# First projection of a perceiver kernel: DMA order, fold products and key loads rearranged

## The reference

```
q_hk  = (layernorm(x) @ Wq.T).reshape(b, s, H, K)          # H=16, K=128
q_big = einsum('bshk,hkq->bshq', q_hk, w_kc_q)             # 192
q_r   = einsum('bshq,hqr->bhsr', q_big, W_qr)              # 64
k_r   = einsum('bld,hdr->bhlr', kv_rope, W_kr)
scores = einsum('bhsr,bhlr->bhsl', q_r, k_r)
...
out = ctx_lat.reshape(b, s, H * K) @ Wo.T
```

## Time and profile before

| | us |
|---|---|
| three runs, median (lowest to highest) | 834.14 (825.74 to 835.28) |
| the profiled execution | 835.64 |
| its span | 833.9 |
| first projection: from the span's start to the first product of the next stage | 78.7 |

### The profile page before, as it was taken

One profiled execution on the slowest core, in us unless ns is written; L12 is line 12 of the kernel. 1 busy time (PEld: TensorE's weight loads), 2 busy tenths in 40 slices (PEclk: granted clock), 3 DMA queues, 4 the chain that ended last, 5 costly groups with the idle time before them and its releaser, 6 DMA issues. The chain is left out here.

```text
span 833.9 us, 16002 instructions
## 1 busy us (share of the span) xinstructions
PE 705.1 (85%) x5490; PEld 471.9 (57%) x5490; DVE 591.0 (71%) x1151; ACT 426.2 (51%) x1314; POOL 369.4 (44%) x312
## 2 busy tenths in 40 slices
PE   4996999788457569899996899769999999999776
PEld 3664666478313345443442577447777776777644
DVE  3456778565778646566675788598888888888477
ACT  1455788244157511222233777326655555668764
POOL 3400454152426313433476544246666676667200
PEclk9999899999569758999999899899999999999999
DMA  8454000000020002252010000002222233231001
GB/s 241 133 150 157 2 2 2 0 2 1 0 89 1 0 21 88 76 164 89 0 39 1 1 1 2 1 20 58 59 57 57 58 99 100 58 107 22 1 1 52
DMA packets 33572, 41.92 MB, mean 50 GB/s; under 512 B 15072, under 2 KB 23264, under 8 KB 32608
## 3 DMA queue, kind: packets, MB, share of 16 engines
q1 hardware_dynamic: 33504, 41.06, 16.8%
HBM read 40.00 MB, written 1.05 MB: 49 GB/s over the span
## 5 line engine op out<-in xcount | busy, mean ns | idle before, releaser
L1918 POOL TENSOR_TENSOR ra_direct<-ra_direct,ra_crossed 128x512 f32<-128x512 f32 x64 | 81.2, 1269 | 80.0 <-DVE ra_crossed L2094 80.0
L695 POOL TENSOR_TENSOR c_probs<-c_probs,c_inverse 128x512 f32<-128x512 f32 x64 | 65.7, 1041 | 74.3 <-DVE c_inverse L711 74.3
L2094 DVE SCALAR_TENSOR_TENSOR ra_crossed<-bank,ra_bias,ra_sin 64x512 f32<-64x512 f32 x128 | 96.0, 750 | 1.9
L1383 POOL TENSOR_TENSOR r_turned<-r_times_a,r_times_b 128x1024 f32<-128x1024 f32 x24 | 56.4, 2350 | 86.2 <-DVE r_times_b L1582 86.2
L670 ACT ACTIVATE c_probs<-bank,c_neg_max 128x128 f32<-128x128 f32 x256 | 90.2, 391 | 5.3 <-DVE c_neg_max L729 5.3
L670 ACT ACTIVATION_READ_ACCUMULATOR c_probs<-bank,c_neg_max 128x1 f32 x256 | 59.4, 232 | 0.0
L2046 ACT ACTIVATE ra_probs_t<-bank 64x256 f32<-64x256 f32 x64 | 24.2, 377 | 59.8 <-PE bank L1988 59.4
L1661 POOL TENSOR_TENSOR ra_w_lo<-ra_raw,ra_w_hi 128x768 f16<-128x768 f32 x32 | 52.7, 1646 | 0.0
L2052 ACT ACTIVATE ra_probs<-ra_masked,ra_neg_max 128x64 f32<-128x64 f32 x128 | 42.9, 336 | 18.5 <-DVE ra_neg_max L2114 18.3
L58 PE MATMUL bank<-xt_hi,ra_w_hi 128*128 128x512 f16 x128 | 49.3, 385 | 1.6 <-DVE ra_crossed L2094 0.9
L621 PE MATMUL bank<-c_probs_t,c_keys 128*64 128x512 f32 x128 | 37.3, 663 | 14.0 <-DVE c_probs_t L721 11.8
(11 more groups left out here) (248 smaller groups left out, 2099.3 us busy)
## 6 DMA issues: line engine op xcount, KB each, us to landing
ra_raw<-l_attn_w_dram SPq DMA_DIRECT2D x32, 384.0 KB, 3.1
wq<-l_wq_dram SPq DMA_DIRECT2D x16, 256.0 KB, 2.9
wo<-l_wo_dram SPq DMA_DIRECT2D x16, 256.0 KB, 3.4
wkcq<-l_wkcq_dram SPq DMA_DIRECT2D x16, 192.0 KB, 3.1
ra_wo<-l_attn_wo_dram SPq DMA_DIRECT2D x1, 2048.0 KB, 9.9
wqr<-l_wqr_dram SPq DMA_DIRECT2D x16, 96.0 KB, 3.3
x_res<-x_dram SPq DMA_DIRECT2D x2, 512.0 KB, 4.7
wkv<-l_wkv_dram SPq DMA_DIRECT2D x16, 64.0 KB, 2.8
```

Source lines behind the costliest of these rows:

```text
L695: nc.gpsimd.tensor_tensor(out=probs[u][:, at, :], in0=probs[u][:, at, :], in1=inverse[u][:, at].unsqueeze(2).broadcast_to([P, HP, L]), op= ...
L1383: nc.gpsimd.tensor_tensor(out=turned[k % 3][:], in0=times_a[k % 2][:], in1=times_b[k % 2][:], op=ALU.add).then_inc(rotated, 1)
L1918: nc.gpsimd.tensor_tensor(out=direct[e][k][:], in0=direct[e][k][:], in1=crossed[k][:], op=ALU.add).then_inc(roped, 1)
L2094: ins = nc.vector.scalar_tensor_tensor(dst[out_lo:out_lo + rows].rearrange("p t (b s) -> p (t b) s", b=2), src[lo:lo + rows], bias[e][lo:l ...
```

## The change

- SyncE loads the weights of pair 0 first, then the two halves of x (each with a semaphore of its own) and the identity, then pair 1.
- Step n of TensorE is now B(n+1), p(n,0), M(n+1), O(n+1), A(n+2), p(n,1). A(1) stands ahead of the steps, behind the first eight transposes; the other eight stand behind p(0,0). ScalarE's and VectorE's orders follow.
- The three loads for the keys stand behind the weights of pair 3, the eleven of the attention weights behind those of pair 4. The first keys are transposed behind step 5 instead of step 1.
- All eight steps are written out; there is no loop any more. VectorE takes the statistics of the first half of x when that half is there, and stores fold product 0 between the two scalings.

```diff
-def pair_loop(eng, step):
...
+def pair_loop(step):
+
+    for n in range(PAIRS):
+        step(n, n % 2, n // 2, n + 1 < PAIRS)
...
-        KEY_GROUPS = {1: (0, 1), PAIRS - 2: (2, 3)}
+        KEY_GROUPS = {PAIRS - 3: (0, 1), PAIRS - 2: (2, 3)}
...
+            for n in range(PAIRS):
+                u = n % 2
                 wait(sp, m_done, n - 1)
                 wait(sp, o_done, n - 1)
                 for dst, name in ((wqr, "l0_wqr"), (wkr, "l0_wkr"), (wkcq, "l0_wkcq"), (wq, "l0_wq"),
                                   (wkv, "l0_wkv"), (wo, "l0_wo")):
                     sp.dma_start(dst[u][:], a[name][n]).then_inc(loaded[u], 16)
-                if isinstance(n, int) and n == 1:
+                if n == 0:
+                    for q in range(2):
+                        rows = slice(q * TH, (q + 1) * TH)
+                        sp.dma_start(m.x[:, rows, :], x_in[:, rows, :]).then_inc(x_loaded[q], 16)
+                    sp.dma_start(m.ident[:], a["ident"]).then_inc(ident_loaded, 16)
+                if n == 3:
                     keys.sync(sp)
+                if n == 4:
                     prep.load(sp)
...
                 if more:
-                    multiply_a(n + 1, v, i + u)
+                    multiply_b(n + 1, v)
                 project(n, u, 0)
+                if isinstance(n, int) and n == 0:
+                    for k in (2, 3):
+                        ln.transpose(pe, k)
                 if more:
-                    multiply_b(n + 1, v)
+                    multiply_m(n + 1, v)
                     multiply_o(n + 1, v)
-                    multiply_m(n + 1, v)
+                if later(n):
+                    multiply_a(n + 2, u, i + 2)
                 project(n, u, 1)
...
-            ln.tensor(pe)
-            pair_loop(pe, step)
+            for k in (0, 1):
+                ln.transpose(pe, k)
+            multiply_a(1, 1, 1)
+            pair_loop(step)
...
-            dve.wait_ge(x_loaded, 32)
-            ln.vector(dve)
+            for q in range(2):
+                dve.wait_ge(x_loaded[q], 16)
+                ln.statistics(dve, q)
+            ln.scale(dve, 0)
+            keep_o(0)
             keep_m(0, 0)
-            keep_o(0)
-            pair_loop(dve, step)
+            ln.scale(dve, 1)
+            for k in (0, 1):
+                ln.low(dve, k)
+            pair_loop(step)
```

More of the change, by code:

```diff
@@ L380, in cross_project_plain, with later @@
         ln = normalise_steps(nc, g, "ln0")
-        x_loaded, ident_loaded = g.sem("x_loaded"), g.sem("ident_loaded")
+        x_loaded, ident_loaded = [g.sem(f"x_loaded{q}") for q in range(2)], g.sem("ident_loaded")
         block = own.enter_context(nc.Block())
+        def later(n):
+            return not isinstance(n, int) or n + 2 < PAIRS
         @block.gpsimd
@@ L405, in step @@
                     sp.dma_start(dst[u][:], a[name][n]).then_inc(loaded[u], 16)
-                if isinstance(n, int) and n == 1:
+                if n == 0:
[4 more added lines that the diff above has]
+                if n == 3:
                     keys.sync(sp)
+                if n == 4:
                     prep.load(sp)
-            pair_loop(sp, step)
             load_ffn_weights(nc, g, sp)
@@ L413, in _, with multiply_a @@
         def _(pe):
-            def multiply_a(n, u, i):
-                pe.wait_ge(loaded[u], 16 * LOADS * (i + 1))
+            def multiply_a(n, u, trips):
+                pe.wait_ge(loaded[u], 16 * LOADS * trips)
                 wait(pe, a_kept, n)
@@ L470, in step @@
                     keys.tensor(pe, KEY_GROUPS[n])
-            multiply_a(0, 0, 0)
+            multiply_a(0, 0, 1)
             multiply_o(0, 0)
@@ L503, in step @@
                 if more:
-                    keep_a(n + 1)
+                    keep_b(n + 1)
                 lat.high(act, n, u, 0)
+                if isinstance(n, int) and n == 0:
+                    for k in (2, 3):
+                        ln.high(act, k)
                 if more:
-                    keep_b(n + 1)
+                    keep_m(n + 1, v)
                     keep_o(n + 1)
-                    keep_m(n + 1, v)
+                if later(n):
+                    keep_a(n + 2)
                 lat.high(act, n, u, 1)
@@ L517, in _ @@
             keep_m(0, 0)
-            ln.scalar(act)
-            pair_loop(act, step)
+            for k in (0, 1):
+                ln.high(act, k)
+            keep_a(1)
+            pair_loop(step)
         @block.vector
```

## The result

Over 20 runs of each, the changed kernel has a median of 836.8 us (833.0 to 843.3), the one before 833.6 (825.7 to 841.1). The ratio is 1.0061, 95% interval 1.0036 to 1.0085: slower by 3.2 us between the medians and by some 5 us by the ratio, which leaves out runs in a slower state of the chip. That is well under 2%, but clear of the noise. A gain of 0.5 us was forecast. The ratios further down are to the kernel before too, with the same kind of interval, each against runs of it that were made beside them.

The account below looks back on a forecast made before the run. TensorE was taken to bound the stage: 3 to 4 us won at the start and 1.6 in the steps, some 5 us lost to load stalls, -0.5 us in sum, median 833.6 us, range 826.5 to 838.5; forecast's chance 0.55.

Parts of the forecast that it names:

- The loads, which are late next: Weight loads released one step (6.04 us) before use need 6.4 us: stalls of 0.3 to 0.4 us every second step.
- The start: Pair 0's weights first: A(0) at 7.2 instead of 10.43, O(1) done at 26.7; 3 to 4 us won.
- The steady step: M's 0.27 us wait for `fold_b` goes, so a step takes 6.04 us instead of 6.31.
- The queue of SyncE: Keys' and attention loads ahead of pair 5 delay its issue to 43.6, though O(3) released it at 39.7.
- The landing of pair 5: Pair 5's loads take 6.4 us from 43.6, so A(5) starts at 50.0 and TensorE waits 3.9 us.
- The forecast's bounds: A wait at A(5) of 2.5 to 6.5 us instead of 3.9, giving -1.9 to +2.1 us.
- Rival 1: The stall between A(5) and A(7) drops TensorE's clock: +2.1 us against before, median 836.2; chance 0.30.
- the 3.02 us ahead of 78.73: Argument against rival 1: TensorE stood 3.02 us before the next stage in the old profile and the clock held.
- The price of 2.6 us: Rival 1's clock cost on the sum: 3.0 us lost at half clock less 0.4 for the covered A(7) wait.
- The sum: Stage ends at 78.2 instead of 78.7, -0.5 us; start and step gains taken back by some 5 us of load stall.

Follow-up runs that it names:

- second profile: Kernel before and changed kernel each run once more with nothing changed: spans 831.0 and 837.3 us, stage ends 76.17 and 86.33.
- old order with late side loads: Kernel before, loop written out, with only the fourteen side loads and first keys moved as in the change: ratio 1.0115, median 839.8 us.
- long fillers: Changed kernel with unread float16 products ahead of late A: 4, 8, 28 and 6 at pairs 3, 4, 5, 7; ratio 1.0033 to the kernel before.
- attention loads last: Changed kernel with only the eleven attention-weight loads put behind the last pair's weights: ratio 0.9975 to the kernel before, median 830.5 us.
- side loads early: Changed kernel with the keys' and attention loads back behind pair 1: ratio 1.0030 to the kernel before, stage end 85.1.
- third set: Changed kernel with a third set of weight buffers, loads released a step earlier: ratio 0.9926 to the kernel before, median 827.4 us.
- short fillers: Changed kernel with 4, 8, 8 and 5 unread float16 products ahead of A at pairs 3, 4, 5, 7: ratio 1.0061 to the kernel before.

## Why the prediction was wrong

The bound of the stage, the new bottleneck and its place were read right: "The loads, which are late next". The sign was not. By its own steps:

- **The start.** A(0) at 7.2 forecast, 7.9 measured in both profiles. The tokens were taken to land near 8.5 and 10 and landed at 10.3 and 13.2 in the first, so the transposes stood at 16.1 and 14.8 in the two profiles instead of about 14, and p(0,0) began at 21.8 in the first instead of 19.5. O(1) was nonetheless done at 27.8 and 26.5 (26.7 forecast), for the clock rose earlier. Where the sum has 3 to 4 us won, p(0,1) began 1.8 and 1.5 us earlier than in the kernel before, with the 0.9 us of A(2) done besides: 2.7 and 2.4.
- **The steady step.** 6.04 forecast, 5.77 measured. Beside the 0.27 of waiting, three starts come closer: from the last product of the second projection to what follows 0.22 instead of 0.31 us, from B to what follows 0.84 instead of 0.93, from O 0.58 instead of 0.65. Undersized, in the good direction.
- **The queue of SyncE** was right almost to the tenth: pair 5's first issue at 43.6 forecast, 43.53 in the second profile and 44.82 in the first, whose TensorE was slowed at A(4); `kcos` held SyncE 1.7 and 1.8 us where 2.6 were taken; O(4) at 46.1 forecast, 46.25 in the second profile.
- **The landing of pair 5, the step that failed first.** "A(5) starts at 43.6 + 6.4 = 50.0" took 3.6 us for `wo`, the median of a quiet stage. It took 5.1 us in the first profile and 7.0 in the second, and A(5) started at 52.67 and 53.34. What the sum left out is the time that the bytes take. It counts SyncE's issues one by one, but 1.9 MB of attention loads and the 0.9 MB of pair 5 are 11.3 us at the 253 GB/s that it uses for the start, and 0.9 MB more of pair 6 make 14.9: from the first attention issue at 36.81 in the second profile that gives 48.1 without pair 6 and 51.7 with all of it, an estimate, against 53.3 measured. In the five profiles that have the late attention loads and two sets of weights, `wo` of pair 5 was issued anywhere from 45.95 to 48.23 and landed from 52.4 to 53.3: an earlier issue bought almost nothing. Pair 6's loads right behind aren't the whole of it, for they stood there too in the old order with late side loads, where `wo` took 4.8 us. No run changed the bytes alone. The forecast's bounds (2.5 to 6.5) took in the trace's longest landing of 5.2, but the wait behind O(4) at full clock is 6 to 7 us.
- **The clock, the step that failed for the rest.** Rival 1 had 0.30 and was what came: low stretches in both profiles of the changed kernel, 13.7 us in each. It was argued down by one row, the 3.02 us ahead of 78.73 behind which the clock held. That row was luck: in the second profile of the same program the clock was low 1.2 us behind the same gap, as in ten of fourteen profiles. The price of 2.6 us measures 3.0 and 4.6. The place was right: the fall that cost something was behind the start of A(5) in the first profile and in the wait ahead of it in the second; the earlier one at A(4) only took the place of waiting. The Trainium skill's rule (TensorE: Matmul & The Clock Gate, The HAM clock gate) that activity releases the throttle spoke for this rival. The windows from 32 to 48 us above agree with it only in part: TensorE was busy from end to end there and stayed at the low level.
- **The sum.** 78.2 was forecast for the end. The kernel with the long fillers, whose clock stays high, has 81.06, and the changed kernel 84.07 and 86.33: the loads' landing is about half of the miss in the first profile, the clock the rest. As a difference, -0.5 us stood for the stage; the profiles show +5.3 and, between the two second ones, +10.2. The first was measured from a base in which the clock rose only at 32 us; in the other four profiles with the old order it had risen by 27.5, and the second profile of the kernel before ends its stage 2.6 us earlier. That the time of 836.8 lies inside the forecast's range (826.5 to 838.5), and near the 836.2 of rival 1, is in part luck: the whole time also holds the spread of what follows the stage.

Not settled: how much of the 3 to 5 us of the whole kernel is which. The stage differences between single profiles scatter by 2 to 3 us and what follows the stage by 7. Whether holding pair 6's loads back would bring pair 5's earlier wasn't tried. What decides how long a low stretch lasts stays open.

## What to carry to other kernels

Moving a product earlier moves the date at which its inputs are due, and the release of the buffers stays where it was: count from the release to the use, with the DMA queue's own work in between, and set the bytes of everything queued against the rate that the trace shows, not only the issues and the median landing of a quiet queue. Loads that nobody needs yet belong behind the last load that somebody waits for, as the eleven attention loads did here. An argument from one row of one profile (the clock held there) is worth a second profile. And where TensorE is the bound, a wait of 1 to 2 us may cost twice: once as a wait, and again because the products behind it run at half clock.

## What the runs showed of the hardware that wasn't expected

- TensorE's clock fell in or behind waits for loads of 1.40 and 1.75 us (changed kernel), 1.55 (attention loads last), 1.72 (side loads early) and 1.87 us (third set) and in or behind the three of 4 to 7 us, and held over others of 0.8 to 1.44 us; the 1.44 is A(7) in the second profile of the changed kernel. Behind the 3.0 us ahead of the next stage it was low within 1.3 us in ten profiles and held for 4.9 to 5.7 us in four.
- The low stretches behind these waits lasted 3.4 us (third set; old order with late side loads), 6.8 to 6.9 (changed kernel; attention loads last), 13.7 (changed kernel, second profile) and 20.5 (side loads early; short fillers). In one of the last two TensorE was busy without an idle moment from 32 to 48 us.
- The first rise of the clock differs between executions of one program: at 32 us and before 27.1 us in the two profiles of the kernel before, which moves the end of the stage by 2.6 us.
- The landing of one 256 KB load ranges from 2.9 to 7.1 us within one stage; it was long where the DMA engines were full (share 0.97, 253 GB/s).
